# Products into an unread PSUM bank in the idle time of TensorE, in all four edge passes of a graph network

## The reference, cut to what is computed

```
x = LN(x + L0(x))   # edge softmax of one score per source row, weighted sum of rows into dst
x = LN(x + L1(x))   # graph attention, 4 heads of 64: softmax over the edges of dst, sum, then an MLP
x = LN(x + L2(x))   # graph convolution: gelu(segment_sum(dinv[src] dinv[dst] h[src]) + b)
x = LN(x + L3(x))   # edge MLP: gelu([x[src], x[dst], w] @ We1 + be1) @ We2 summed into dst, then a node MLP
```

## Time and profile before

| | |
|---|---|
| median of three timed runs | 10232.7 us (10225.35 to 10239.77) |
| the profiled execution | 10246.39 us, its span from first to last instruction 10244.6 us |
| mean granted TensorE clock | 0.682 |
| busy: TensorE, VectorE, ScalarE, GpSimd | 52%, 50%, 23%, 60% of the span |

### The profile page before, as it was taken

One profiled execution on the slowest core, in us unless ns is written; L12 is line 12 of the kernel. 1 busy time (PEld: TensorE's weight loads), 2 busy tenths in 40 slices (PEclk: granted clock), 3 DMA queues, 4 the chain that ended last, 5 costly groups with the idle time before them and its releaser, 6 DMA issues. The chain is left out here.

```text
span 10244.6 us, 122678 instructions
## 1 busy us (share of the span) xinstructions
PE 5291.4 (52%) x27385; PEld 4421.4 (43%) x27385; DVE 5160.7 (50%) x11723; ACT 2355.6 (23%) x7991; POOL 6141.6 (60%) x6667
## 2 busy tenths in 40 slices
PE   1544444447366655655673333333346666666665
PEld 1434343336244544444552322222235555555553
DVE  4644544446466666666652222222235555555556
ACT  1212221225244444444460000000012111111114
POOL 5666666662555655655515666666656666666665
PEclk8665656657677777778786666566667666666667
DMA  4111111113444444444421111111113333333331
GB/s 108 46 46 47 46 47 47 47 46 95 94 99 99 100 97 98 99 97 99 97 66 42 46 45 44 45 46 46 46 48 115 102 102 102 102 102 103 101 102 46
DMA packets 873481, 770.05 MB, mean 75 GB/s; under 512 B 386905, under 2 KB 731984, under 8 KB 872389
## 3 DMA queue, kind: packets, MB, share of 16 engines
q0 software_dynamic: 229872, 527.55, 19.2%
q1 hardware_dynamic: 626723, 228.61, 9.2%
q10 hardware_dynamic: 16184, 6.05, 0.2%
HBM read 707.25 MB, written 54.31 MB: 74 GB/s over the span
## 5 line engine op out<-in xcount | busy, mean ns | idle before, releaser
L978 POOL DMA_INDIRECT rows_h<-t_d,idx x1563 | 1479.2, 946 | 1038.2 <-PE pn_h L1118 446.9
L579 POOL DMA_INDIRECT rows_sum<-t_d,idx x1532 | 1445.1, 943 | 1049.1 <-issue 433.1
L579 POOL DMA_INDIRECT rows_mlp<-t_d,idx x1548 | 1468.3, 949 | 810.0 <-issue 412.8
L978 POOL DMA_INDIRECT rows<-t_d,idx x1491 | 1410.0, 946 | 791.8 <-issue 408.2
L1118 PE MATMUL pn_h<-S_h,rows_h 128*128 128x128 f32 x6252 | 1122.9, 341 | 281.1 <-ACT rows_h L1017 123.1
L1118 PEld LDWEIGHTS pn_h<-S_h,rows_h 128*128 128x128 f32 x6252 | 1050.9, 251 | 445.9 <-issue 416.5
L776 DVE TENSOR_TENSOR big<-big,pn_sum 128x512 f32 x391 | 269.2, 688 | 1746.4 <-remote 1358.0
L1017 ACT ACTIVATE rows_h<-rows_h,wc_h 128x64 f32<-128x64 f32 x4688 | 1139.5, 333 | 28.3 <-issue 17.6
L624 PE MATMUL pre_mlp<-dw_mlp,ST_mlp 128*128 128x128 f32 x3126 | 676.7, 380 | 404.8 <-issue 151.8
L631 PE MATMUL pn_sum<-zb_sum 128*128 128x512 bf16 x391 | 220.2, 563 | 1242.9 <-DVE big L776 779.1
L624 PEld LDWEIGHTS pre_mlp<-dw_mlp,ST_mlp 128*128 128x128 f32 x3126 | 596.0, 282 | 459.3 <-issue 455.5
(11 more groups left out here) (358 smaller groups left out, 8557.2 us busy)
## 6 DMA issues: line engine op xcount, KB each, us to landing
dw_mlp<-bd_d SPq DMA_DIRECT2D x1563, 64.0 KB
frow_sum<-t_d SPq DMA_DIRECT2D x2048, 0.5 KB
frow_sum<-t_d ACTq DMA_DIRECT2D x1920, 0.5 KB
frow_mlp<-t_d ACTq DMA_DIRECT2D x1920, 0.5 KB
lrb_h<-lrrow_d SPq DMA_DIRECT2D x196, 128.0 KB
lrb_mlp<-lrrow_d SPq DMA_DIRECT2D x98, 256.0 KB
rows_h<-t_d,idx POOLq DMA_INDIRECT x1563
dw_h<-xp_d SPq DMA_DIRECT2D x1563, 3.0 KB
```

Of the source, the lines that this page charges most:

```text
L579: e.indirect_dma_start(rows[:, g % NR, j, :], None, table, bass.IndirectOffsetOnAxis(ap=idx[:, b, t:t + 1].bitcast(I32), axis=0)).then_inc ...
L978: e.indirect_dma_start(rows[:, g % NR, j, :], None, table, bass.IndirectOffsetOnAxis(ap=idx[:, b16, t:t + 1].bitcast(I32), axis=0)).then_i ...
```

## The change

A new helper `stay_awake` writes the product of the identity matrix with itself, repeated over the 512 columns of a bank, with `start` and `stop` set, so that nothing is accumulated. It is issued on TensorE's stream:

- in sum and mlp behind the placing of each group but the last two, four times in sum and twice in mlp, into a new PSUM bank `spare`;
- in soft at the end of each group's turn (but the last two), three times, into `spare`;
- in gat before each of the two clearings of a group, once each, into the bank that is then cleared; the first of them takes over the wait on `s_add`.

Nobody reads `spare`. No wait, DMA or instruction of another engine is added.

```diff
+AWAKE = {"soft": 3, "gat": 1, "sum": 4, "mlp": 2}
...
+def stay_awake(e, spare, ident, n):
+
+    for _ in range(n):
+        w = spare.shape[1]
+        e.matmul(spare, ident[:, :], ident[:, :].unsqueeze(1).broadcast_to([P, w // P, P]), start=True, stop=True)
...
+        spare = ps("spare", [P, 512])
...
                 place(g, r0[4 * q:4 * q + 4])
+                if g < GR - 2:
+                    stay_awake(e, spare[:, :], c["ident"], AWAKE["mlp" if mlp else "sum"])
...
+        spare = None if gat else ps("spare", [P, 512])[:, :]
...
                 for k in range(blocks):
+                    if gat:
+                        stay_awake(e, pn[g % 2][:, k, :], ident, AWAKE["gat"])
                     e.matmul(pn[g % 2][:, k, :], zb[:, 0:P], zb[:, :], start=True, stop=False)
...
                 if gat and i + AHEAD < GR:
                     expand(i + AHEAD)
+                if not gat and i < GR - 2:
+                    stay_awake(e, spare, ident, AWAKE["soft"])
```

## The result

The changed kernel is slower: 10404.8 us (median of four runs, 10395.7 to 10424.0) against 10230.2 for the kernel before beside it, a ratio of 1.0162 (95% interval 1.0142 to 1.0181). Its profiled execution has a span of 10397.3 us, 152.7 more than before. The predicted 10353 us was 52 us too low, the sign was right and the size roughly so; of its terms for the four passes two came near (gat, mlp) and two did not (soft, sum).

The account below looks back on a forecast made before the run. GpSimd's gathers, with a backlog that delays TensorE's messages, were taken to bound the four passes. Terms of +5 soft, +70 gat, +25 sum and +20 mlp made +120 us on the median 10232.7, so 10353 us, range 10130 to 10600.

Parts of the forecast that it names:

- GpSimd's gathers pace all passes, not TensorE: All four edge passes: GpSimd's gathers set the pace, 5.0 us for a group of four, and the rest is stops.
- Late messages belong to the gathers, not to the clock: TensorE's done messages queue behind gathers, 9 and 17 us late; stops cost 0.5 us plus 0.15 us a gather.
- Soft, +5: Pass soft: three products at a turn's end, covered by idle time and the faster clock; +5 us, bounds 0 and +110.
- Gat, +70: Pass gat: two products before a group's clearing delay its placing and transposes; +70 us, bounds -230 and +350.
- The fifth of 0.9 us: Pass gat: of 0.9 us more TensorE work a group, a fifth gets through, 0.18 x 391 = +70 us.
- Sum, +25: Pass sum: four products fit in the group's time; 21 us for single rows, 4 for shorter runs; bounds 0 and +120.
- the one on single rows: Pass sum: after 14 waits for single rows, products delay the next placing; 1.5 us each, 21 us.
- Mlp, +20: Pass mlp: two products between placing and expanding, nearly repaid by the faster clock; +20 us, bounds -30 and +120.
- Price of a product, 0.96 us: TensorE: one 128x512 f32 product takes 0.96 us at full clock, 2.00 us at half.
- The clock pays: Rival, chance 0.27: in gat, transposes and placings at full clock outweigh the products; -100 us, 10130.
- Runs become short: Rival, chance 0.13: fewer groups are reported, so GpSimd stops after every group, or TensorE is the bound; +450 us, 10680.
- The tells with fixed numbers: Clock above 0.9 in sum and soft; paces within 0.1 us a group of 5.78 (soft), 5.87 (sum), 5.88 (mlp).

Follow-up runs that it names:

- the slowed GpSimd: Kernel before, without products, with GpSimd clearing a small unread tile behind each gather in sum and mlp: ratio 0.9998.
- the fourth chip: Chip where the kernel before took 8553.8 us and the changed kernel 8626.5 us, ratio 1.0088; products in gat alone took 8573.4 us.
- the second chip: Products in one pass alone against the kernel before (10367.7 us): soft 10451.6, gat 10487.3, sum 10350.1, mlp 10375.9 us.
- set 3: Runs on the fourth chip, among them the kernel before with sum's ring cut from 8 groups to 2, meant to test SyncE's issues: 8592.6 us.
- the third: Chip where the changed kernel without products in each pass's last groups took 10351.3 us, ratio 1.0105 to the kernel before (10245.7 us).
- the kernel with eight: Eight products a group in pass sum and none elsewhere, against the kernel before: 11098.7 us, +853.

## Why the prediction was right, and where it was not

- **GpSimd's gathers pace all passes, not TensorE.** Right, by the slowed GpSimd, by the pace that stayed while the clock rose by 0.12 to 0.33, and by the fourth chip. But I called the stops a price of the gathers, as if each stop were paid by itself. They are only how GpSimd meets a pace set behind it (1.47 us a gather in mlp, where GpSimd alone takes 1.25): some 220 us of stops were turned into work for 8 us of time.
- **Late messages belong to the gathers, not to the clock.** Right. The length of a stop after 8 and after 16 gathers is the same at full clock (medians of 1.88 and 2.94 us beyond the usual 0.30 in sum, against 1.8 and 3.0 in the earlier trace rows, from which I had 0.5 us plus 0.15 a gather). What this leaves out is the chip: on the fourth there are no such stops.
- **Soft, +5.** It was +77 (+73 on the second chip, +52 on the fourth), inside the bounds, but the value was wrong by 72 us. Two steps failed. I took the products at the end of a turn as covered wherever TensorE is idle, but 45 stops in place of 32 wait truly for TensorE, 86 us in place of 48. On the second chip this growth (92 us in place of 51 to 58) is nearly all of the 41 us that the gathers lose. And I summed by groups only and left out the pass's end, where 32 gathered groups wait and nothing covers TensorE: +36.5 us, and +52 on the fourth chip, where it is nearly all of the loss.
- **Gat, +70.** It was +64 (+119 and +21 on the second and fourth chip). The mechanism (products in front of the group's own placing, some of it through) was right. The fifth of 0.9 us that I let through had no row behind it, so the near hit is luck, as the other two chips show; and 11 of the 64 us are the pass's end, which I had left out here too.
- **Sum, +25.** It was -22.5, outside the bounds. The step that failed is the one on single rows: I read the earlier trace rows as a place where TensorE's lateness would be added, while it was SyncE that ended last. Before, SyncE issued a tile's 128 rows in 139 us, 24 groups passed in 141, and TensorE placed each such tile within 3 us of the last row's issue: pass sum was held by SyncE as much as by GpSimd. In rows (SyncE's issues, and TensorE's products of all 31 fetched tiles, SyncE's 16 among them: count, ns, first and last start; before, then after, then what is left of TensorE's wait):

```profile
L506 SPq DMA_DIRECT2D frow_sum<-t_d x2048: 2/228/1453, 5354.8 to 7563.7; - x187
...
L644 PE MATMUL pn_sum<-S_sum,frow_sum x62: 275/421/577, 5488.8 to 7566.4; 128*128 128x128 f32 x62
...
L515 SPq DMA_DIRECT2D frow_sum<-t_d x2048: 2/202/1398, 5523.5 to 7409.9; - x187
...
L653 PE MATMUL pn_sum<-S_sum,frow_sum x62: 275/275/574, 5640.3 to 7700.2; 128*128 128x128 f32 x62
...
  DMA frow_sum<-t_d: 8.4, 1
```

  Before, SyncE's last row was issued at 7563.7 and placed at 7566.4. After, it was issued at 7409.9 and placed at 7700.2; TensorE waited for such rows once in the pass, for 8.4 us. With four products GpSimd stops more often after 8 gathers (88 times in place of 2) and seldom after 16 (10 times in place of 39), and SyncE takes 107 us for a tile. That the first brings the second is shown in part only, as said in set 3. The gain itself is in the traces of three chips: -22.5, -32 and, from first to last gather on the third, 2244.9 us against 2277.6 to 2283.9. The lower bound of 0 for this pass had no reason behind it.
- **Mlp, +20.** It was +8 (+7 on the second and -1 on the fourth chip).
- **Price of a product, 0.96 us.** It is 0.86 back to back. The higher price put the turning point at 4.7 products in place of 5.5, and the expected time of the kernel with eight 350 us too high.
- **Rivals.** The clock pays: it was granted, 0.89 to 0.95, and 1.00 in gat, sum and mlp on the fourth chip, and no pass but sum gained, where the waits for SyncE's rows went. Runs become short: they did (170, 328 and 163 stops in place of 137, 277 and 119), but since a short run's stop is short too, the price is small. The tells with fixed numbers held for mlp and sum (paces within 0.1 us) and just failed for soft (5.80 to 5.91, by whole spans).

The rule of the Trainium skill that I weighed (TensorE: Matmul & The Clock Gate, "Why this matters for your kernels") is right here on what the clock does: with the idle time filled it rose from 0.59 to 0.77 up to 0.89 to 0.95. It speaks of TensorE's own speed and not of what that brings to a kernel: the eight instructions that place a group's four tiles take 1.05 us at full clock and 1.91 at half, and soft, gat and mlp took no less time for it.

## What to carry to other kernels

Filling an engine's idle time to raise its clock is worth what that engine's speed is worth on the path, and it is not free at the end of a loop over a ring, where the feeder is done and the filled engine drains the ring alone. Before pricing a wait, look at what ended last for it: of the waits that looked like TensorE's here, one kind was a backlog behind GpSimd and one was SyncE's issues. Whether an engine's stops are a cost or only the pace of what it feeds is tested by making that engine slower.

## What the runs showed of the hardware that was not expected

- One chip of four, in the one set of runs on it, took GpSimd's indirect DMAs as fast as they were issued, one in 1.25 us. The others took one in 1.45 to 1.51 us over whole passes (gat aside) with the same instructions of 0.946 us, and there TensorE's messages came up to 17 us late. That is 8554 against 10230 to 10368 us for the same kernel. GpSimd's own time for a gather and the DMA time per MB (0.70 and 0.73%) are the same, so I suspect what lies between; no run here says where.
- SyncE's issue of single rows shares this: 51 us for 128 rows without a backlog, 55 where GpSimd stops 3 us in each group, 107 to 141 with it. In the trace of before its rate falls from 1.8 to 0.5 rows a microsecond as GpSimd's run of gathers grows.
- The effect of a change can depend on the chip: the changed kernel lost 175 us on the first and 73 on the fourth, and the same kernel with products in gat alone lost 119 us in that pass on the second and 21 on the fourth.
